# Keys of four units projected ahead in fp32, and the experts' first gathers issued in the routing

## What is computed

```python
xn = _layernorm(x)
# attention: 16 heads of 16, each block of 64 queries sees its own and the previous block (band of 64)
qkv = xn @ w_qkv                                   # 256 x 768
attn = softmax(where(band, q @ k.T / 4, -1e30))
a = (attn @ v) @ w_out
# experts: 8 experts, 2 per token, 1024 rows each
scores = softmax(xn @ wg); topv, topi = top_k(scores, 2)
h = relu(gathered(xn) @ w1[e] + b1[e]); y = h @ w2[e] + b2[e]
x + a + sum_k gate_k * y[slot_k]
```

## Time and profile before

| what | value |
|---|---|
| median of 3 runs | 733.26 us (733.17 to 733.62) |
| profiled execution | 732.93 us, of which the span of the profile is 731.1 us |
| busy share of the span | PE 94%, PEld 82%, DVE 61%, ACT 62%, POOL 52% |
| mean granted TensorE clock | 0.965 of full |

### The profile page before, as it was taken

How to read it: one execution, slowest core, us unless ns; L and a number is a source line. 1 busy time by engine, 2 the same in 40 slices (tenths; PEclk the granted TensorE clock), 3 DMA queues, 4 the chain that set the end, 5 groups by cost and what they waited for, 6 DMA issues and landing times. The chain is left out here.

```text
span 731.1 us, 19852 instructions
## 1 busy us (share of the span) xinstructions
PE 684.1 (94%) x6849; PEld 599.4 (82%) x6849; DVE 449.0 (61%) x1680; ACT 452.2 (62%) x1459; POOL 379.2 (52%) x543
## 2 busy tenths in 40 slices
PE   5654899999999999999999999899999999999987
PEld 3443689899898998989989888788888888898976
DVE  7984343543534425344253441689989898989895
ACT  4552570844807439165292560888979898888892
POOL 4556460543514525246153310578668677588774
PEclk7976799999999999999999999899999999999999
DMA  9734031142222422224223001432436354534332
GB/s 306 271 115 156 27 112 56 65 143 86 91 67 72 136 93 78 80 72 129 60 72 119 23 12 50 132 89 86 116 103 165 84 151 117 143 91 122 109 107 75
DMA packets 59056, 76.44 MB, mean 105 GB/s; under 512 B 9448, under 2 KB 51560, under 8 KB 58984
## 3 DMA queue, kind: packets, MB, share of 16 engines
q1 hardware_dynamic: 52488, 58.69, 25.5%
q0 software_dynamic: 6144, 16.79, 8.1%
q10 hardware_dynamic: 352, 0.04, 0.0%
HBM read 51.81 MB, written 17.03 MB: 94 GB/s over the span
## 5 line engine op out<-in xcount | busy, mean ns | idle before, releaser
L1101 ACT ACTIVATE a_p<-a_p,a_nmax 128x128 f32<-128x128 f32 x512 | 198.1, 392 | 33.0 <-DVE a_nmax L1140 32.5
L750 DVE TENSOR_TENSOR m_hl<-m_hf,m_hh 128x512 fp32r<-128x512 f32 x128 | 93.2, 728 | 100.0 <-ACT m_hh L707 100.0
L66 PE MATMUL m_psY<-m_w2h,m_hh 128*128 128x256 f32 x512 | 145.1, 283 | 0.0
L66 PE MATMUL m_psY<-m_w2l,m_hh 128*128 128x256 f32 x512 | 143.9, 281 | 0.0
L66 PE MATMUL m_psY<-m_w2h,m_hl 128*128 128x256 f32 x512 | 143.8, 281 | 0.0
L703 ACT ACTIVATE m_hf<-m_psF,b1T 128x512 f32<-128x512 f32 x128 | 88.1, 688 | 66.5 <-PE m_psF L66 52.0
L1140 DVE CUSTOM_DVE_ANT_0 a_p<-a_psS,mask 128x128 f32<-128x128 f32 x512 | 117.4, 286 | 15.6 <-PE a_psS L1265 15.0
L671 POOL CAST m_w2h<-raw 128x256 fp32r<-128x256 f32 x64 | 25.9, 405 | 178.2 <-PE m_psY L66 120.6
L66 PE MATMUL m_psF<-m_xh,w1h 128*128 128x512 f32 x256 | 103.6, 405 | 1.9 <-DVE m_xl L727 1.9
L66 PE MATMUL m_psF<-m_xl,w1h 128*128 128x512 f32 x256 | 102.0, 399 | 0.0
L66 PE MATMUL m_psF<-m_xh,w1l 128*128 128x512 f32 x256 | 102.0, 398 | 0.0
(11 more groups left out here) (200 smaller groups left out, 1357.7 us busy)
## 6 DMA issues: line engine op xcount, KB each, us to landing
raw<-in_L_ffn_w SPq DMA_DIRECT2D x16, 1024.0 KB, 5.4
y_scratch<-y SPq DMA_DIRECT2D x64, 128.0 KB, 1.7
n_xin<-in_L_attn_x SPq DMA_DIRECT2D x8, 512.0 KB, 7.8
xn_scratch<-n_xn SPq DMA_DIRECT2D x8, 512.0 KB, 7.0
a_res<-in_L_attn_x SPq DMA_DIRECT2D x8, 512.0 KB, 4.7
a_rall<-recip_scratch SPq DMA_DIRECT2D x31, 128.0 KB
xnr<-xn_scratch SPq DMA_DIRECT2D x7, 512.0 KB, 5.5
out<-a_res SPq DMA_DIRECT2D x7, 512.0 KB, 3.7
```

The source lines that it names most:

```text
L66: last = pe.matmul(out, a, b, start=(n_start and i == 0), stop=(n_stop and i == n - 1))
L750: dve.tensor_tensor(hl[:, u // HC, u % HC, :], hf[:, u % FR, :], hh[:, u // HC, u % HC, :].bitcast(fp32), ALU.subtract).then_inc(hl_done, 1)
L1101: act.activation(e, e, ACT.Exp, scale=-1.0, bias=nmax[:, r, j:j + 1], accum_out=sums[:, r, j:j + 1]).then_inc(exp_done, 1)
```

## The change

The keys of units 4 to 7 (two tiles of 128 columns each, eight in all) leave the attention's passes 3 to 6. They are computed in route_phase, each by two plain fp32 matmuls (raw_qkv by the slots of n_xT, which now lives as m.xT until the routing's end), copied from PSUM by ACT (six) and DVE (two) and stored to DRAM by SP, 256 KB each. In passes 3 to 6 SP loads 512 KB of them into kT right behind the halo. A second plan of shares is used from pass 3 on. In the routing POOL scales three rows of a group and ACT nine; values run one group ahead. The first four gathers stand at the end of POOL's routing queue behind a semaphore on token_of. The load of xnr moves to the last expert and expert 1's w1 waits for the first transposes. Not shown: allocations, and the places that take bank_for[w, i] where they took i % 2.

```diff
@@ norm_phase @@
-        xT = sb("n_xT", [P, C + 1, KD, G * P], fp32)
-        T_OF = lambda n: n if n <= C else n - C
+        xT, T_OF = m.xT, m.xT_slot
@@ route_phase @@
-        BY_DVE, BY_POOL, BY_ACT = slice(0, 4), range(4, 9), range(9, R)
+        BY_DVE, BY_POOL, BY_ACT = slice(0, 4), range(4, 7), range(7, R)
...
+        KEYS = KD * len(m.early_k)
+        K_DVE = (5, 7)
+        kst = sb("r_kst", [P, KEYS, L // 2], fp32)
...
+        psK = [ps(f"r_psK{i}") for i in range(3)]
+        k_done, k_copied = sem("r_k_done"), [sem(f"r_k_copied{i}") for i in range(3)]
@@ route_phase, sync @@
+        def key_copied(ins, n):
+            ins.then_inc(k_copied[n % 3], 1)
...
+            def keys_out(n):
+                sp.wait_ge(k_copied[n % 3], n // 3 + 1)
+                sp.dma_start(m.k_dram[n], kst[:, n, :]).then_inc(m.k_out, 16)
...
+            for n in range(4):
+                keys_out(n)
...
+            for n in range(4, KEYS):
+                keys_out(n)
@@ route_phase, gpsimd @@
+            pool.wait_ge(m.tokens, 1)
+            for j in range(ST // 2):
+                pool.indirect_dma_start(m.xg[j][:, :], None, xn_dram,
+                                        bass.IndirectOffsetOnAxis(ap=m.token_of[:, j:j + 1], axis=0))\
+                    .then_inc(m.xg_in[j], 16)
@@ route_phase, scalar @@
+            def key_copy(n):
+                act.wait_ge(k_done, n + 1)
+                key_copied(act.activation(kst[:, n, :], psK[n % 3][:, :], ACT.Copy), n)
...
+            key_copy(0)
+            key_copy(1)
...
+                if n % 2:
+                    key_copy(2 + n // 2)
@@ route_phase, scalar and tensor @@
+            for n in range(4, KEYS):
+                if n not in K_DVE:
+                    key_copy(n)
...
+            def keys(n, terms=range(KD)):
+                unit, j = m.early_k[n // KD], n % KD
+                if n >= 3 and terms[0] == 0:
+                    pe.wait_ge(k_copied[n % 3], n // 3)
+                for k in terms:
+                    ins = pe.matmul(psK[n % 3][:, :], m.raw_qkv[:, k, D + j * P:D + (j + 1) * P],
+                                    m.xT[:, m.xT_slot(unit), k, :], start=k == 0, stop=k == KD - 1)
+                if terms[-1] == KD - 1:
+                    ins.then_inc(k_done, 1)
...
+            keys(0)
+            keys(1)
@@ route_phase, tensor @@
+                if n % 2:
+                    keys(2 + n // 2)
...
-            for g in range(C // R):
...
+            def values(g):
...
+            values(0)
+            for g in range(C // R):
+                if g + 1 < C // R:
+                    values(g + 1)
...
+                if g < KD:
+                    keys(4, (g,))
...
+            for n in range(5, KEYS):
+                keys(n)
@@ route_phase, vector @@
-            link(dve.scalar_tensor_tensor(m.token_of[:, :], tab_ps[:, 0:E * ST], float(P), tabp[:, :],
-                                          ALU.mult, ALU.add))
+            dve.scalar_tensor_tensor(m.token_of[:, :], tab_ps[:, 0:E * ST], float(P), tabp[:, :], ALU.mult, ALU.add)\
+                .then_inc(m.tokens, 1)
+            for n in K_DVE:
+                dve.wait_ge(k_done, n + 1)
+                key_copied(dve.tensor_copy(kst[:, n, :], psK[n % 3][:, :]), n)
@@ moe_phase, sync @@
-            ut = L // 2 // P
-            sp.dma_start(m.xnr[:, :, :], xn_dram.rearrange("(t p) d -> p t d", p=P)[:, ut:2 * ut, :])\
-                .then_inc(xnr_in, 16)
...
-                if not last:
...
+                if last:
+                    ut = L // 2 // P
+                    sp.dma_start(m.xnr[:, :, :], xn_dram.rearrange("(t p) d -> p t d", p=P)[:, ut:2 * ut, :])\
+                        .then_inc(xnr_in, 16)
+                else:
...
+                    alone(sp, t_done, e * TG + KD)
...
-                for j in range(ST):
+                for j in range(ST // 2 if first else 0, ST):
...
+            dve.wait_ge(m.k_out, 16 * KD * len(m.early_k))
@@ attention_phase @@
-    SHARE = [4, 0, 4, 4, 4, 4, 4, 4] + [3] * 8
-    parts_at, done_at = [[] for _ in range(STEPS)], [[] for _ in range(STEPS)]
-    at, spent = 0, 0
-    for i, (kind, _) in enumerate(ITEMS):
-        for part in range(PARTS[kind]):
-            while at < STEPS - 1 and spent >= sum(SHARE[:at + 1]) - 1e-6:
-                at += 1
-            parts_at[at].append((i, part))
-            spent += COST[kind]
-        done_at[at].append(i)
...
+    def plan(kinds, share):
+        parts_at, done_at = [[] for _ in range(STEPS)], [[] for _ in range(STEPS)]
+        at, spent = 0, 0
+        for i, (kind, _) in enumerate(ITEMS):
+            if kind not in kinds:
+                continue
+            for part in range(PARTS[kind]):
+                while at < STEPS - 1 and spent >= sum(share[:at + 1]) - 1e-6:
+                    at += 1
+                parts_at[at].append((i, part))
+                spent += COST[kind]
+            done_at[at].append(i)
+        return parts_at, done_at
...
+    PLANS = (plan("xqkvo", [4, 0, 4, 4, 4, 4, 4, 4] + [3] * 8),
+             plan("xqvo", [4, 0, 3, 3, 3, 3, 3, 3] + [3, 2, 2, 2, 2, 2, 2, 3]))
...
+    def plan_of(w):
...
+        return PLANS[1 if w + 1 >= m.early_k[0] else 0]
...
+        if ITEMS[i][0] == "k" and w + 1 in m.early_k:
+            return False
...
-    count, before = {}, [PRO // 2] * 2
+    count, bank_for, before = {}, {}, [PRO // 2] * 2
...
+        n = 0
...
-                count[w, i] = before[i % 2]
-                before[i % 2] += 1
+                bank_for[w, i] = n % 2
+                count[w, i] = before[n % 2]
+                before[n % 2] += 1
+                n += 1
...
-                [(g // STEPS, i) + ITEMS[i] for i in done_at[g % STEPS] if present(g // STEPS, i)]
+                [(g // STEPS, i) + ITEMS[i] for i in plan_of(g // STEPS)[1][g % STEPS] if present(g // STEPS, i)]
...
+            sp.wait_ge(m.k_out, 16 * KD * len(m.early_k))
@@ attention_phase, sync @@
+                    if w + 1 in m.early_k:
+                        n = m.early_k.index(w + 1) * KD
+                        sp.dma_start(kT[1 - u][:, :, WIN:WIN + UL], m.k_dram[n:n + KD].rearrange("j p t -> p j t"))\
+                            .then_inc(k_in, 16)
@@ attention_phase, tensor @@
-                    for k in ((V_FIRST - 2, V_FIRST - 1) if w == 0 else (V_FIRST - 1,)):
-                        pe.wait_ge(item_free[k % 2], k // 2 + 1 if w == 0 else count[w - 1, k] + 1)
+                    if w == 0:
+                        for k in (V_FIRST - 2, V_FIRST - 1):
+                            pe.wait_ge(item_free[k % 2], k // 2 + 1)
+                    elif w in m.early_k:
+                        pe.wait_ge(k_in, 16 * (m.early_k.index(w) + 1))
+                    else:
+                        pe.wait_ge(item_free[bank_for[w - 1, V_FIRST - 1]], count[w - 1, V_FIRST - 1] + 1)
@@ build @@
+        m.early_k = range(4, 2 * B)
+        m.k_dram = nc.dram_tensor("k_scratch", (KD * len(m.early_k), P, tokens), fp32, kind="Internal").ap()
+        m.k_out = ctx.enter_context(nc.semaphore("k_out"))
...
+            m.xg = [inner.enter_context(nc.sbuf_tensor(f"xg{j}", [P, D], fp32)) for j in range(ST)]
+            m.xg_in = [inner.enter_context(nc.semaphore(f"xg_in{j}")) for j in range(ST)]
+            m.tokens = inner.enter_context(nc.semaphore("tokens"))
...
+                m.xT = early.enter_context(nc.sbuf_tensor("xT", [P, 5, KD, tokens], fp32))
+                m.xT_slot = lambda n: n if n <= 4 else n - 4
```

More of the change, by code:

```diff
@@ L588, in moe_phase @@
         idx = sb("m_idx", [P, ST], u32)
-        xg = [sb(f"m_xg{j}", [P, D], fp32) for j in range(ST)]
+        xg, xg_in = m.xg, m.xg_in
         xh, xl = sb("m_xh", [P, KD, CAP], fp32r), sb("m_xl", [P, KD, CAP], fp32r)
@@ L599, in moe_phase @@
         idx_done = sem("m_idx_done")
-        xg_in = [sem(f"m_xg_in{j}") for j in range(ST)]
         t_done = sem("m_t_done")
@@ L905, in attention_phase @@
         shift_in = m.shift_in
-        halo_in = sem("a_halo_in")
+        halo_in, k_in = sem("a_halo_in"), sem("a_k_in")
         pads = sem("a_pads")
@@ L973, in freed @@
                 for i in last_two:
-                    sp.wait_ge(item_free[i % 2], count[w, i] + 1)
+                    sp.wait_ge(item_free[bank_for[w, i]], count[w, i] + 1)
             def store(w):
@@ L1006, in _ @@
                 j = ITEMS[i][1]
-                sp.wait_ge(item_free[i % 2], count[UNITS, i] + 1)
+                sp.wait_ge(item_free[bank_for[UNITS, i]], count[UNITS, i] + 1)
                 sp.dma_start(ov[:, LAST_U * UT + j:LAST_U * UT + j + 1, :], res[LAST_U % 2][:, j:j + 1, :])\
@@ L1054, in _ @@
                     if kind == "q":
-                        pool.wait_ge(item_free[i % 2], count[w, i] + 1)
+                        pool.wait_ge(item_free[bank_for[w, i]], count[w, i] + 1)
                         for s in range(2):
@@ L1075, in read_item @@
             def read_item(w, i, kind, j):
```

(8 more changed lines are left out.)

## The result

724.02 us, the median of 4 runs (723.59 to 724.51), against 733.21 us for the kernel before beside it (731.78 to 733.62): a ratio of 0.9871, 95% interval 0.9859 to 0.9882. The forecast was 723.6 us, faster. The profiled execution took 723.59 us, its span 721.71.

The account below looks back on a forecast made before the run. TensorE's queue was taken to bound attention passes 3 to 6. From the profiled 732.93, minus 11.2, plus 2.8, minus 1.3 gave 723.2, hence a median of 723.6 us; range 719.0 to 728.5, the forecast's own 720.5 to 726.

Parts of the forecast that it names:

- The removed products: Attention passes 3 to 6: 48 key matmuls at 0.23 us leave TensorE, 11.2 us in all, 2.8 a pass.
- The load ahead of the reciprocals: SP's queue, passes 3 to 6: the 512 KB load delays the broadcast by 2.0 us, costing 2.8 in all.
- bound of 4.5: Attention: the most the passes lose to the delayed broadcast, if broadcasts land as slowly as in pass 5; at least 1.8.
- The second plan only redistributes what is left: Attention shares: 1.4 us less TensorE work before step 8; o starting some steps earlier was given no cost.
- the prediction's own sign: Attention passes 3 to 6: the prediction is wrong if PE waits elsewhere than before L1153 and for L1167 in step 8.
- DVE as the bound: Rival, attention: a pass keeps DVE's idle 3.14 us and ends at 32.0, gaining only 1.4; 726.6 us, chance 0.12.
- The other rivals: All hidden 719.5 (0.18); keys 5 to 7 at half clock 729.5 (0.06); load whole first 738.8 (0.05); fp32 products uncovered 738.7 (0.02).
- the slower outcome: Rival, attention: the load stands whole before the reciprocals, 5.5 us; 738.8 us, decisive from 4.1 us of delay; chance 0.05.
- The price of a key: Routing: two fp32 matmuls of two 0.43 us records each make 1.73 us a key, 13.8 us for eight.
- ACT's two rows more: Routing: ACT is 1.3 us later if it ends last; the table is then 1.7 late, bounds 0 and 5.2.
- The experts' start: Routing's end to first expert matmul: early gathers bring it forward by 0.6 to 1.9 us; 1.3 taken.
- keys 5 to 7 are hidden: Behind the table: 5.2 us of keys, a copy and the meeting end at 73.0, just hidden; at half clock 78.2.

Follow-up runs that it names:

- load_behind_first_group: Changed kernel with the 512 KB key load moved behind the residual's load and the first group's own reciprocals: 723.5 us, ratio to before 0.9870.
- start_alone: Changed kernel with all keys back in the attention, without key products, copies, stores and loads in the routing: 729.9 us, ratio to before 0.9955.
- split_back: Changed kernel with the rows of one-hot tiles split as before, POOL five and ACT seven: 727.1 us, ratio to before 0.9911.
- two_gathers: Changed kernel with only two of the first four gathers in the routing, the other two behind the meeting: 726.3 us, ratio to before 0.9908.
- load_twice: Changed kernel with a second 512 KB load into an unread spare buffer right behind the first: 734.4 us, ratio to before 1.0004.
- load_behind_recips: Changed kernel with the 512 KB key load moved behind the reciprocals' broadcast, still ahead of the residual's load: 722.0 us, ratio to before 0.9841.
- recips_plan_late: As load_behind_recips, with two units of share moved from steps 6 and 7 to steps 12 and 13: 722.4 us, ratio to before 0.9846.

## Why the prediction was right, and where its steps were not

**The removed products: right.** 11.2 us for 48, or 2.8 a pass. Where no wait stands, a pass takes 30.66 against 33.40, which is 2.74.

**The load ahead of the reciprocals: right, in mechanism and in size.** The delay was put at 2.0 us; halo to broadcast grew by 1.9, 1.8, 2.7 and 1.6 in passes 3 to 6, so 2.0 on the mean. The Trainium skill (DMA: Bandwidth & Descriptors, Queues, rings and completion order) has the descriptors of one issuer taken in ring order on each DMA engine; these runs agree. The estimate of 1.5 us from the table in the Bandwidth section of that page of the Trainium skill lies below the measurement. The order of the passes came out too, pass 5 the longest. By the starts of the same instructions in load_behind_first_group's pass 3, which has no wait, step 8 lost 0.52, 0.51 and 1.63 in passes 3 to 5. That is 2.7, where 2.8 was summed (the list of waits counts from the modelled ends and has 2.1), and the load behind the broadcast gave 2.6 back (166.84 to 164.26).

But the loss in the attention is 11.2 - 6.4 = 4.8, not 2.8, and over the bound of 4.5. Another 1.5 lie at the x transposes of passes 4 to 6, some 0.5 are spread over passes 3 to 5 in steps too small to place, and 0.2 is the price of a pass (2.74, not 2.8).

**The step that failed: "The second plan only redistributes what is left".** That o starts earlier was counted as nothing, and the 1.5 us at the x transposes are its price; the prediction's own sign, that PE waits elsewhere in these passes, came up. The light steps put the output's additions where PE has least to do. There a step takes DVE about 1.8 us (copy 0.6, addition 0.33, four maxima at 0.21), more with a multiply or reciprocals; PE's steps, 30.66 / 16 = 1.9 us on the mean, are shorter there. In the changed kernel DVE has no idle time from 583 to 587 us, and the next pass's x transposes wait for its last addition (DVE, then PE):

```profile
584.88 0.41 DVE L1201 TENSOR_TENSOR a_res<-a_res,a_psA 128x256 f32<-128x256 f32 x1
...
586.05 0.69 DVE L1249 COPY a_pT<-a_psP 128x512 f32<-128x512 f32 x1
586.65 0.41 DVE L1201 TENSOR_TENSOR a_res<-a_res,a_psA 128x256 f32<-128x256 f32 x1
...
587.12 0.66 PE L1307 MATMUL a_psA<-eye,xnr 128*128 128x128 f32 x4 [0.33 <-DVE a_res L1201]
```

Neither place of the load removed these waits; the later shares did.

**DVE as the bound.** That rival named 32.0 us a pass, and the mean of passes 3 to 5 is (31.3 + 31.6 + 33.1) / 3 = 32.0. As a bound of the pass it is wrong all the same: with the loads moved and the later shares the same DVE work fits in 30.7 to 31.2. It holds only in the light steps, as above. A rival's number can be hit by other causes; only the waits tell.

**The other rivals.** Nothing in the changed kernel's profile speaks for them: the load is not hidden; the keys behind the table ran at the full clock (twelve records in 5.37 us); the delay stayed at 2.7 us or less where the slower outcome began at 4.1; and the fp32 products were covered but for 2.3 + 1.0 us.

**The routing: one sign wrong, one term too small.** The price of a key held (eight records of keys 0 and 1 in 3.67 us, at the full clock), and so did the cover before L471. But the table came 0.7 earlier, not 1.7 later. The keys were summed at 0.45 and cost 2.3: their copies do not all lie in ACT's waits. Those of keys 2 and 3 stand ahead of ACT's rows of the first group, which begin 17.3 us behind the normalisation's last transpose, against 15.0 in start_alone. Against this stands a gain of 3.0 without the keys, where a loss of 1.3 was summed for ACT's two rows more. The engine that ended last was POOL (3.01 us of wait for it in the earlier trace rows), and its two rows fewer are worth 0.8 by split_back. How the rest divides between the reordered values and the clock is open: in the kernel before, TensorE was granted half its clock for the first two groups' products (PEclk in the line below; 16 of them took 1.90 us), while the changed one had the full clock from 20.6 to 71.8 (1.18 us).

```profile
52.00:58.00 6.00, 4.82 (x39) 4.75 (x39) 3.81 (x4) 3.74 (x18) 3.81 (x8) 0.50 0.00 1
```

**The experts' start: a gain of the right size from other terms.** 1.3 was forecast. Without the normalisation's chance the first matmul gained 0.69 + 0.56 = 1.25, and 0.84 came inside the experts from the clock, which was not a term and scatters between the kernels (see the last section). That keys 5 to 7 are hidden held; what hid them was POOL's drain, which ended 3.6 us behind them and was not in the forecast. What the moved loads of xnr and w1 give was not tried by itself.

So that the sum came within 0.4 us is luck: a loss in the attention 2.0 too small met gains at the start that were 1.7 too small (0.86 of them chance in the normalisation, 0.84 the clock).

## What to carry to other kernels

When a load joins a queue that also carries a latency-critical round trip, price it by what stands behind it, and put it behind that round trip if its reader is a pass away. When work leaves the bounding engine, check step by step which engine is slowest in the thinned steps; a mean over the pass hides it. DMAs issued ahead of a meeting of engines gain only until that meeting waits for their landing. And look at the granted clock of a stretch before its time is put down to waits alone.

## What the hardware showed unexpectedly

POOL's queue drains at a block's end only when its indirect DMAs have landed: by the semaphores' times in the traces the drain ends 0.21 us behind the last of these landings in eleven kernels and 0.13 in two_gathers. Counted from the end of the last issue that is 2.0 to 2.1 us without key stores beside them, 2.9 to 3.4 with 256 KB stores, and 4.1 in load_twice; two gathers fewer end it 2.1 us earlier.

The reciprocals' broadcast, mostly 2.7 to 3.1 us from issue to landing, took 4.1 to 5.5 us in pass 5 of four kernels, and 3.8 before. In all five it was issued 7.9 to 8.0 us behind the halo; issued at 5.9 us, or from 8.3 us on, it took 2.8 to 3.1, but for one at 9.1 (3.4). Pass 2's, ahead of the first key load, shows the same: 3.5 to 4.5 us in the seven kernels that issued it at 7.5 to 7.8. Which transfer it met at that moment was not settled.

How long TensorE stays at 1.2 GHz behind the first expert matmul varied from 2.9 us (load_behind_recips) to 6.1 (recips_plan_late) between two kernels whose code up to the attention is the same. By my estimate (half of the difference) this alone is worth up to 1.6 us.
